# One load of a tile's sizes, a semaphore per step and a ring of 192 slots in the small graph-attention aggregation

## The reference

```python
x = x + gnn0(layernorm(x), edges)                  # 8 heads x 32
x = x + ffn0(layernorm(x), ffn_edges)              # this case's stage
x = x + gnn1(layernorm(x), edges)                  # 4 heads x 64
x = x + ffn1(layernorm(x))                         # 8 experts, best 2

# inside ffn0, 131072 edges, 4 heads x 4:
e = leaky_relu(a_src[src] + a_dst[dst], 0.2)
ee = exp(e - segment_max(e, dst)[dst])
alpha = ee / (segment_sum(ee, dst)[dst] + 1e-16)
agg = segment_sum(h[src] * alpha[:, :, None], dst)
# best 2 of 4 experts by layernorm(agg); every expert: gelu(x @ W1 + b1) @ W2 + b2
```

## Time and profile before

| what | us |
|---|---|
| median of 3 runs (lowest, highest) | 10248.09 (10223.0, 10260.06) |
| the profiled execution's own time | 10220.8 |
| its span, first to last instruction | 10218.8 |
| PE, DVE, ACT, POOL busy | 2312.4, 5655.7, 1171.8, 5738.3 |
| the small aggregation within the span | 4250 to 5809 |

### The profile page before, as it was taken

The page is one execution under the profiler, slowest core; times in us unless marked ns, Lnnn a source line. Parts: engine busy times, 40 slices in busy tenths (PEclk is TensorE's granted clock), DMA queues, the critical chain, the costliest instruction groups (busy, mean ns, idle before and its releaser), DMA issues. The chain is left out here.

```text
span 10218.8 us, 56607 instructions
## 1 busy us (share of the span) xinstructions
PE 2312.4 (23%) x9111; PEld 1766.1 (17%) x9112; DVE 5655.7 (55%) x8530; ACT 1171.8 (11%) x2978; POOL 5738.3 (56%) x5411
## 2 busy tenths in 40 slices
PE   0112000000000012256555421000000000029995
PEld 0111000000000001145444311000000000026663
DVE  8764688898777667333333474666656465431111
ACT  0101001000000001022222101000000000002221
POOL 0026667677777754545555446777777777542221
PEclk9555555555555555577777755555555555559997
DMA  1052333433333363311111253343343333530004
GB/s 33 0 154 61 91 83 90 119 100 101 99 100 99 93 125 60 113 27 33 28 28 28 69 151 101 103 121 106 108 120 104 111 100 102 123 111 30 30 30 116
DMA packets 485751, 869.30 MB, mean 85 GB/s; under 512 B 202782, under 2 KB 322508, under 8 KB 475840
## 3 DMA queue, kind: packets, MB, share of 16 engines
q0 software_dynamic: 239536, 575.99, 22.6%
q1 hardware_dynamic: 178976, 148.53, 5.3%
q10 hardware_dynamic: 67108, 143.54, 4.2%
HBM read 693.35 MB, written 180.71 MB: 86 GB/s over the span
## 5 line engine op out<-in xcount | busy, mean ns | idle before, releaser
L891 POOL DMA_INDIRECT agg_ring<-table,agg_idx x4320 | 4675.1, 1082 | 2070.6 <-issue 1316.7
L1022 DVE TENSOR_TENSOR agg_part<-agg_ring,agg_prob 128x2048 f32 x420 | 960.9, 2288 | 160.5 <-DVE agg_wide L1058 76.1
L1058 DVE TENSOR_TENSOR agg_wide<-agg_wide,agg_part 128x2048 f32<-128x2048 f32 x420 | 962.7, 2292 | 14.4
L1036 DVE TENSOR_TENSOR agg_score<-agg_el,agg_er 128x576 f32<-128x576 f32 (+1 forms) x98 | 59.8, 610 | 1268.9 <-issue 661.9
L1389 PE MATMUL agg_hp<-agg_xt,agg_w 128*128 128x256 f32 x1600 | 462.5, 450 | 555.7 <-ACT agg_ht L1359 267.4
L2205 DVE TENSOR_TENSOR experts_h<-experts_sg,experts_hp 128x682 f32<-128x682 f32 x106 | 91.8, 866 | 779.4 <-ACT experts_sg L2188 779.4
L2155 PE MATMUL experts_hp<-mixture_w,experts_xt 128*128 x1696 | 517.8, 457 | 0.6 <-ACT experts_xt L2184 0.6
L2126 POOL DMA_INDIRECT yc<-experts_ysb,experts_list x105 | 103.9, 990 | 684.3 <-DVE experts_ysb L2214 684.3
L1389 PEld LDWEIGHTS agg_hp<-agg_xt,agg_w 128*128 128x128 f32 x1600 | 361.3, 229 | 643.6 <-issue 298.5
L1403 PE MATMUL agg_yp<-agg_w,agg_ht 128*128 128x256 f32 x1600 | 408.0, 414 | 231.1 <-remote 141.4
L1962 PE MATMUL agg_weights_turned<-all_ident,agg_n 128*128 128x128 f32 x192 | 48.5, 406 | 1677.1 <-issue 827.3
(11 more groups left out here) (418 smaller groups left out, 6360.8 us busy)
## 6 DMA issues: line engine op xcount, KB each, us to landing
agg_ring<-table,agg_idx POOLq DMA_INDIRECT x4320
y<-agg_ysb ACTq DMA_DIRECT2D x25, 1024.0 KB
rank_y<-y SPq DMA_DIRECT2D x10, 2560.0 KB
rank_x<-x SPq DMA_DIRECT2D x30, 640.0 KB
copies<-first_sort_words SPq DMA_DIRECT2D x16, 1024.0 KB
copies<-last_sort_words ACTq DMA_DIRECT2D x16, 1024.0 KB
x<-rank_x SPq DMA_DIRECT2D x20, 640.0 KB
agg<-agg_res ACTq DMA_DIRECT2D x98, 128.0 KB
```

The source lines that it names most:

```text
L891: pool.indirect_dma_start(out=self.ring[:, at:at + self.RW], out_offset=None, in_=self.table, in_offset=bass.IndirectOffsetOnAxis(ap=self. ...
L1022: return dve.tensor_tensor(to[:, :].rearrange("p (j h c) -> p j h c", j=UNIT, h=H), ring[:, ds(st.at(at_u), UNIT * RW)].rearrange("p (j w) ...
L1058: dve.tensor_tensor(wide[:, :], wide[:, :], part[:, :], ALU.add).then_inc(widened, 1)
```

## The change

It touches the small aggregation and the ring size of list 1.

- DVE copies the four tables of sizes of all tiles into one table `sizes`, once (`lay_sizes`, 4 copies; the function is now shared with the large aggregations, which already did this). Each tile then loads its four sizes with one load on DVE, without the checks of the single loads; ACT does the same in place of its two loads.
- `acc` and `den` are cleared once; a tile's first chunk scales what is there by the factor exp(-1e30 - maximum), which is 0. The maximum is still reset per tile. The wait for the tile before (L1201) goes.
- Each step of the chain has its own semaphore, which counts chunks; all waits of a chunk use the one value `kk`, or two or three times it. 15 semaphores come and 2 go. The row sum now waits only for the weighing. At a chunk's end come waits for three steps.
- The ring of list 1 has 192 slots: 12 entries, 12 index tiles, 12 semaphores of each kind; POOL's and SP's loops have 12 entries written out. Rings are counted in 192 slots.

```diff
+def lay_sizes(dve, st, sizes, sized):
+    of_tile = sizes[:, :].rearrange("p (t w) -> p t w", w=4)
+    for w, first in enumerate((I_NG, I_NK, I_C0, I_K0)):
+        dve.tensor_copy(of_tile[:, :, w], st.inf[:, first:first + NT]).then_inc(sized, 1)
+    dve.wait_ge(sized, 4)
+
+
+def sizes_of(nc, cfg, sizes, eng, t):
+    why = "the ranking bounds every size of a tile"
+    ng, nk, c0, k0 = nc.values_load_multi_w_load_instructions(sizes[0:1, ds(t * 4, 4)], engines=[eng.engine], min_val=0, max_val=cfg.max_slots,
+                                                              skip_runtime_bounds_check_because=why)[1]
+    return nc.s_assert_within(ng, UNIT, CH, skip_runtime_bounds_check_because=why), nk, c0, k0
...
@@ aggregate_small, DVE @@
-                    ng, nk, c0, k0 = st.tile(dve, t)
+                    ng, nk, c0, k0 = sizes_of(nc, cfg, sizes, dve, t)
+                    done = t + 1 if isinstance(t, int) else dve.snap(t + 1)
                     dve.wait_ge(st.ready, st.entries((c0 + ng) >> 3))
-                    dve.wait_ge(tile_done, t + 1)
...
-                    dve.memset(acc[:, :], 0.0).then_inc(tstep, 1)
-                    dve.memset(den[:, :], 0.0).then_inc(tstep, 1)
-                    dve.wait_ge(tstep, t * TS + TS)
+                    dve.wait_ge(begun, t * 2 + 2)
...
-                        kk = k0 + k
-                        c = kk * CS
+                        kk = dve.snap(k0 + k + 1)
...
-                        dve.wait_ge(cstep, c + 3)
-                        dve.scalar_tensor_tensor(out=sc3, in0=sc3, scalar=0.2, in1=sc3, op0=ALU.mult, op1=ALU.max).then_inc(cstep, 1)
-                        dve.wait_ge(cstep, c + 4)
+                        dve.wait_ge(added, kk)
+                        dve.scalar_tensor_tensor(out=sc3, in0=sc3, scalar=0.2, in1=sc3, op0=ALU.mult, op1=ALU.max).then_inc(leaked, 1)
+                        dve.wait_ge(leaked, kk)
...
-                        dve.wait_ge(cstep, c + 12)
-                        dve.tensor_tensor(den[:, :], den[:, :], dsum[:, :], ALU.add).then_inc(inverted, 1)
-                        dve.tensor_reduce(summed[:, :], weighted[:, :].rearrange("p (j w) -> p w j", j=SJ), AX.X, ALU.add).then_inc(inverted, 1)
+                        dve.wait_ge(weighed, kk)
+                        dve.tensor_reduce(summed[:, :], weighted[:, :].rearrange("p (j w) -> p w j", j=SJ), AX.X, ALU.add).then_inc(folded, 1)
+                        dve.wait_ge(scaled, kk * 3)
+                        dve.tensor_tensor(den[:, :], den[:, :], dsum[:, :], ALU.add).then_inc(dens, 1)
...
+                        dve.wait_ge(kept, kk)
+                        dve.wait_ge(dens, kk)
+                        dve.wait_ge(combined, kk)
+                        dve.sem_inc(st.dve_passed, 1)
...
@@ aggregate_small, ACT @@
-                    nk = act.value_load(st.inf[0:1, ds(t + I_NK, 1)], min_val=1, max_val=cfg.max_slots)
-                    k0 = act.value_load(st.inf[0:1, ds(t + I_K0, 1)], min_val=0, max_val=cfg.max_slots)
+                    _, nk, _, k0 = sizes_of(nc, cfg, sizes, act, t)
...
-        (Cfg("1", 131072, 1024, 96), a["L0_ffn_edge_index"][1], a["L0_ffn_edge_index"][0], N - 1, 4, 4),
+        (Cfg("1", 131072, 1024, 192), a["L0_ffn_edge_index"][1], a["L0_ffn_edge_index"][0], N - 1, 4, 4),
```

More of the change, by code:

```diff
@@ L985, in aggregate @@
         prob_scale = prob[:, SC:SC + H]
[L987 to L991, removed]
         with nc.Block() as block:
@@ L1009, in _ @@
                 dve.wait_ge(st.info_in, 16)
-                of_tile = sizes[:, :].rearrange("p (t w) -> p t w", w=4)
-                for w, first in enumerate((I_NG, I_NK, I_C0, I_K0)):
-                    dve.tensor_copy(of_tile[:, :, w], st.inf[:, first:first + NT]).then_inc(sized, 1)
+                lay_sizes(dve, st, sizes, sized)
                 dve.wait_ge(const, 4)
-                dve.wait_ge(sized, 4)
                 dve.sem_inc(taken, cfg.RU)
@@ L1105, in tile @@
                 def tile(t, share=None):
-                    ng, nk, c0, k0 = sizes_of(act, t)
+                    ng, nk, c0, k0 = sizes_of(nc, cfg, sizes, act, t)
                     own = (c0 % cfg.RS) * RW
@@ L1162, in aggregate_small @@
         ring, taken = st.ring, st.taken
+        sizes, sized = s.sb("sizes", [1, 4 * NT], I32), s.sem("sized")
         er, m, bm, mn = s.sb("er", [P, H]), s.sb("m", [P, H]), s.sb("bm", [P, H]), s.sb("mn", [P, H])
@@ L1167, in aggregate_small @@
         prob = s.ps("prob", [P, 512])
-        const, tstep, cstep, tail = s.sem("const"), s.sem("tstep"), s.sem("cstep"), s.sem("tail")
+        const, begun, masked, tail = s.sem("const"), s.sem("begun"), s.sem("masked"), s.sem("tail")
+        added, leaked, topped, raised, lowered, kept = [s.sem(n) for n in ("added", "leaked", "topped", "raised", "lowered", "kept")]
+        weighed, scaled, dens, folded, combined, floored = [s.sem(n) for n in ("weighed", "scaled", "dens", "folded", "combined", "floored")]
         scored, probs, blank = s.sem("scored"), s.sem("probs"), s.sem("blank")
@@ L1234, in tile @@
+                        dve.wait_ge(raised, kk)
+                        dve.tensor_tensor(score[:, SC:SC + H], m[:, :], mn[:, :], ALU.subtract).then_inc(lowered, 1)
                         dve.tensor_tensor(sc3, sc3, mn[:, :].unsqueeze(1).to_broadcast([P, SJ, H]), ALU.subtract).then_inc(scored, 1)
[L1235 to L1237 removed]
+                        dve.wait_ge(lowered, kk)
@@ L1257, in tile @@
+                    if not (isinstance(t, int) and t == 0):
+                        dve.wait_ge(out_stored, t * 16)
                     dve.tensor_tensor(res[:, :].rearrange("p (h c) -> p h c", h=H), acc3,
                                       den[:, :].unsqueeze(2).to_broadcast([P, H, C]), ALU.mult).then_inc(tile_done, 1)
-                dve.wait_ge(const, 2)
+                dve.wait_ge(const, 4)
                 dve.wait_ge(ffn.weights_in, ffn.nweights * 16)
```

66 lines of the change are left out of this document (31 added, 35 removed).

## The result

The change makes the kernel slower: 10,495.69 us median (10,481.98 to 10,507.15, four runs) against 10,246.83 us for the kernel before on the same chip, a ratio of 1.0246 with a 95% interval of 1.0231 to 1.0262. The profiled execution of after has a span of 10,505.4 us against 10,218.8. Forecast were 10,268 us and a range that ended at 10,370.

The account below looks back on a forecast made before the run. It took the loop through DVE, ACT and PE to set the stage's pace, no engine being full. Terms -94 + 78 + 28 + 8 = +20 us on the 10,248 median gave 10,268 us, range 10,150 to 10,370.

Parts of the forecast that it names:

- One load of the sizes: DVE's passage between tiles in the small aggregation: 4.59 us falls to 1.6, giving -94 us on the 42 later tiles.
- The first stream: POOL's unbroken gathers at the stage's start last to about 4559 with ring 192, three tiles behind: +78 us, bounds 50 to 104.
- from 4281 to 4559 that is 5.6 tiles: Step pricing the lengthened initial gathers: DVE does a tile in 45 to 50 us while they run.
- Streams that merge: Later in the stage, a faster DVE closes two more gaps between POOL's streams of 16 gathers: +28 us, bounds 0 and 70.
- Small items: Table copies, index loads, semaphore clearing, ranking of empty slots, and waits at the chunk's end: 8 us together, rounded up.
- the last gather would come ahead of the stage's end: With ring 192 the 96 extra gathers cost nothing at the end; the last again comes some 75 us before it.
- The slow rival: POOL's long streams and closing gaps slow DVE and PE: +122 us, 10,370 us; chance of more than 0.5% slower 0.33.
- One sign: DVE's wait for PE in the stage would rise from 134 us to 180 or more.
- The circle: Pace-setting loop of the stage: DVE's bias sums, the odd tile's passage and scores, ACT's exponentials, gelus, PE, bias sums again.
- The faster one: Slow stretches follow DVE's instructions and their place, not POOL's stream: -126 us, about 10,122 us; chance of over 0.5% faster 0.30.
- The rule behind it: Taken branches outside a small window stall for code, so slowness shrinks with the shorter loop and the longer first stream costs nothing.
- the load would be taken apart: Rival: DVE's one load of the sizes is split into four, giving +114 us; chance 0.03, within the slower 0.33.

Follow-up runs that it names:

- chip B: Chip of the second kind, where the kernel before takes 9,490 us; the control was traced on it.
- the control: Kernel before with only constant masks on a tile's sizes (some 3 register steps a tile in the large aggregations), ring 96: ratio 0.9994 on chip B.
- C: Chip of the second kind; the kernel after (ring 192, all new code) with constant masks on a tile's sizes took 9,587.41 us there, ratio 1.0102.

## Why the prediction was wrong

**One load of the sizes, -94 us: right in size, wrong in what it is worth.** Passages are 1.44 and 0.69 us (1.6 forecast), the idle ahead of the first copy 88.0 us (about 120 forecast). But no run shows a gain of the stage from it. With the load alone the stage is 1,568.7 us against 1,551.1 on the same chip for the new code with four loads (and 1,513.7 for before on another chip), and on chips of the second kind it is hidden, since DVE waits for gathers there (0.9998).

**The first stream, +78 us, bounds 50 to 104: right mechanism, too small.** Alone, the ring costs 129 us up to the fifth tile. The passages in the stream shrank as I had put it (7.32 and 4.71 us, "about 8"). The step that failed is "from 4281 to 4559 that is 5.6 tiles": three were done. The timeline of DVE, before and then after, shows what I left out:

```profile
4337.38 0.50 DVE L1218 COPY agg_chunk<-agg_ring  x1 [10.83 <-issue]
```

```profile
4302.60 0.18 DVE L1211 COPY agg_er<-agg_ring 128x4 f32 x1 [7.32 <-issue]
4313.14 0.47 DVE L1224 COPY agg_chunk<-agg_ring  x1 [10.36 <-issue]
...
4506.50 1.35 DVE L1244 TENSOR_TENSOR agg_weighted<-agg_chunk,agg_prob 128x1152 f32<-128x1152 f32 x1 [134.13 <-issue]
```

DVE's own part came out as forecast: the passage shrank, the next copy waits as before (10.36 and 10.83 us), and from the first tile's result to the second's it is 42.6 us (4295.04 to 4337.64) in place of 72.8, against my 45 to 50. But I scaled from this, when the circle through ACT and PE had just begun to slow; the third tile's weighting waited 134 us, behind four gelus ahead of which ACT stood idle for 58, 21, 66 and 22 us. A stretch in which PE issued 0.63 matmuls a microsecond gave the better price: at 64 a tile that is 100 us for each, close to three tiles in 296 us.

**Streams that merge, +28 us, bounds 0 to 70: the term that decided.** I wrote "I take two more such gaps". There were 17 (25 joins against 8), and from the fifth tile on the stage was 141 us longer. That is 8.3 for each, net of what the new code saves; if it saved the 94 us forecast, a join cost 13.8, near the 14 that I had read for one. The runs don't part the two. I had seen both halves, that DVE frees units closer together and that a stream outlasts 16 gathers if it does, and never put the two times side by side: a stream of 16 lasts 20 us, the two entries of a round were freed some 24 us apart, and I was about to take 3 us off the passage and more off the chain between them. The passages behind it had kept the second tile's copies in the slow part of the stream and so behind its end. A threshold was taken for a slope.

**Small items, +8 us,** are below what these runs resolve. That the last gather would come ahead of the stage's end held on the first kind of chip (5979.17 against a last result at 6033.69) and fails on the second, by 121 us.

**The sum.** +20 forecast; measured +249 between the medians and +258.9 in the stage. The slow rival had the mechanism and its place, but its price (+122) rested on five joins, and on a saving of 60 us that no row gave. One sign failed that bears on the mechanism: DVE's wait for PE was to rise from 134 us to 180 or more and fell to 98. The circle is the one that I had named, but DVE meets it at the weighting, ahead of ACT's exponentials (525.4 us against 95.3), and not at the bias sums.

**The rivals.** The faster one, that slow stretches belong to places in the loop, is refuted: with pauses in POOL the same code runs its first 139 us with 282 matmuls in place of 88, and on chip B without any pause with 400. The rule behind it (the Trainium skill, "Runtime: NRT & Kernel Launch", section "Instruction fetch mechanics") makes a taken branch out of a small window wait for a fetch. Here the waits are not at branches: from 4300 to 4398 DVE's sequencer ran 71 instructions before, 2 of them branches, and loads, moves, semaphore and register steps took 0.70 us alike in the median; on chip B, in the first 110 us of its tiles, the median is 0.05. Nor are they waits for code. The transfers of instructions in the whole stage before (packets, MB, share of the DMA engines; from 4259 to 5773) are

```profile
q14 instruction: 5, 0.04, 0.0%
q8 instruction: 2, 0.03, 0.0%
```

and 6 in the control on B. So the rule doesn't account for these stalls; the measurement decides. That the load would be taken apart fell with the passages of 1.44 us.

**What stays open:** why streams slow the other engines on some chips and not on others. The program, the gathers' interval and, nearly, the mean granted clock of the launch (0.602 and 0.613) are the same. The traces show what is slow, steps of the sequencers of DVE, ACT and SP and the issue of PE's matmuls, and no cause. Whether it is POOL's issuing of gathers or the transfers that follow from it that slows them isn't told apart either: every pause took both away. And the runs show a difference that goes with the chip's number, three chips and two, and nothing of what else may go with it.

## What to carry to other kernels

An idle time on a fast engine may be what gives a shared resource its pause. Before shortening a passage, set the new distance between two releases beside the time in which the released work runs: where it drops below, short bursts join into long ones, and where long bursts slow others, what this costs has to be priced per joined burst, with the count taken from those distances and not guessed. And a stage that ends with a ring of empty slots pays for a deeper ring where the filler is the bound, as on C (97 us for 96 gathers).

## What was not expected of the hardware

- Whether a stream of gathers on POOL slows the other sequencers depends on the chip: the same kernel before took 10,258 to 10,334 us on three chips and 9,490 to 9,495 on two, of which the stage has 429 us (1,513.7 against 1,084.9 in the control); the other stages were not looked into. A judgement from a single chip would have had the ring and the code at 1.0246 where the other kind gives 1.0102, and a rest at 0.9798 where it gives 1.0169.
- On the first kind, 2.45 us of memset on POOL after every 16 gathers, 132 us of added work, took 2.0% off the launch (0.9798). The stage, 1,307 us, is still far from the 1,085 of the second kind.
- While a long stream ran there, each step of DVE's sequencer took 0.70 us in the median, whatever it was, against 0.05 on chip B.
